# A fp32 graph-convolution kernel: two more convolution products taken in pairs of taps, and the low part of x made on GpSimd

## The reference

```python
h = relu(bn1(conv1d(xc, conv1_w)))              # one tap
h = bn2(conv1d(h, conv2_w, pad=8))              # 17 taps along the nodes
x_conv = relu(h + xc)
s = x @ w_se.T + b_se                           # 3 numbers a node
dist = sq[:, :, None] + sq[:, None, :] - 2 * s @ s.T
A = exp(-dist) * mask
x_nmp = A @ relu(x @ w_msg.T + b_msg)
x_in = concat([x_conv, x_nmp])
r, z = sigmoid(x_in @ w_ih + x @ w_hh ...)      # a GRU cell
n = tanh(gi_n + r * gh_n)
out = layernorm(x + (1 - z) * n + z * x)
```

## Time and profile before

| | us |
|---|---|
| median of 3 runs | 299.93 |
| lowest, highest | 299.28, 303.88 |
| the profiled execution, its own time | 299.77 |
| its span, first to last instruction | 297.9 |
| one round of the loop (first residual transpose to the next round's, 68.55 to 138.38) | 69.8 |

### The profile page before, as it was taken

How to read it: one execution, slowest core, us unless ns; L and a number is a source line. 1 busy time by engine, 2 the same in 40 slices (tenths; PEclk the granted TensorE clock), 3 DMA queues, 4 the chain that set the end, 5 groups by cost and what they waited for, 6 DMA issues and landing times.

```text
span 297.9 us, 4862 instructions
## 1 busy us (share of the span) xinstructions
PE 290.2 (97%) x1464; PEld 238.2 (80%) x1464; DVE 230.5 (77%) x648; ACT 198.7 (67%) x441; POOL 24.2 (8%) x50
## 2 busy tenths in 40 slices
PE   8999999999999999999999999999999999999992
PEld 6787787888887988888887888887888898887881
DVE  2799899599969966459979986449978996625795
ACT  2889656488866678378775769368884759715444
POOL 3100000000000240000000070000000033000113
PEclk9999999999999999999999999999999999999998
DMA  7502436422003323702213122721211041420002
GB/s 251 217 0 74 142 141 185 169 70 66 23 32 97 111 86 98 265 12 67 70 35 106 69 72 85 247 91 70 70 35 35 0 141 70 119 93 0 2 35 106
DMA packets 12257, 27.23 MB, mean 91 GB/s; under 512 B 1363, under 2 KB 2133, under 8 KB 12117
## 3 DMA queue, kind: packets, MB, share of 16 engines
q1 hardware_dynamic: 11956, 26.03, 26.2%
q10 hardware_dynamic: 288, 1.05, 1.1%
HBM read 22.88 MB, written 4.19 MB: 91 GB/s over the span
## 4 chain that ended last, share of the span: by engine, by line
PE 92%; DVE 4%; ACT 1%; issue 1%; POOL 1%; POOLq 0%; DVEq 0%
PE bank L357 89%; PE bank L615 2%; PE bank L410 1%; DVE first L1302 1%; DVE xr L1514 0%; DVE xr L1519 0%; ACT hn L938 0%; DVE first L1308 0%; POOL rstd L1018 0%; DVE xn L1315 0%; POOLq L84 0%; POOL rstd L1065 0%; DVE hn L1507 0%; DVE hn L1331 0%; ACT z L935 0%
## 5 line engine op out<-in xcount | busy, mean ns | idle before, releaser
L357 PE MATMUL bank<-x_hi,w_hl 128*128 128x512 f32 (+1 forms) x122 | 44.5, 405 | 0.0
L357 PE MATMUL bank<-ec_hi,w_hl 128*128 128x512 f32 (+1 forms) x98 | 35.7, 391 | 0.0
L357 PE MATMUL bank<-m_hi,w_hl 128*128 128x512 f32 (+1 forms) x98 | 35.4, 394 | 0.0
L357 PE MATMUL bank<-V_hi,cw_hi 128*128 128x512 f32 x68 | 28.6, 421 | 0.3 <-ACT bank L790 0.3
L357 PEld LDWEIGHTS bank<-x_hi,w_hl 128*128 128x128 f32 x122 | 23.0, 188 | 5.3 <-DVE x_lo L1160 0.5
L357 PE MATMUL bank<-V_lo,cw_hi 128*128 128x512 f32 x68 | 27.2, 399 | 0.0
L357 PE MATMUL bank<-V_hi,cw_lo 128*128 128x512 f32 x68 | 27.1, 398 | 0.0
L1499 DVE SCALAR_TENSOR_TENSOR hn<-xr,hn 128x512 f32<-128x512 f32 x15 | 10.4, 691 | 18.4 <-ACT hn L926 18.4
L1016 POOL TENSOR_TENSOR rstd<-first,pconst 128x4 f32<-128x4 f32 x15 | 3.4, 229 | 260.7 <-DVE first L1308 260.7
L357 PE MATMUL bank<-x_lo,w_hl 128*128 128x512 f32 (+1 forms) x61 | 23.8, 391 | 0.0
L790 ACT ACTIVATE bank<-bank 128x512 f32<-128x512 f32 x24 | 13.6, 581 | 15.1 <-PE bank L357 10.7
(11 more groups left out here) (165 smaller groups left out, 750.0 us busy)
## 6 DMA issues: line engine op xcount, KB each, us to landing
adj<-adj_dram SPq DMA_DIRECT2D x16, 512.0 KB, 4.9
x<-xt_dram SPq DMA_DIRECT2D x16, 256.0 KB, 3.2
xn<-xn_dram SPq DMA_DIRECT2D x16, 256.0 KB, 4.8
...
```

What stands on the lines that cost most here:

```text
L357: return nc.tensor.matmul(out, lhs, rhs, start=start, stop=stop, skip_group_check=True)
```

## The change

1. F2 and F3 (n = 7, 8) are split as E1 and E3 are, in the groups after the first. `T_hi`, `T_lo` get four slots, `V_hi`, `V_lo` keep two. `third(g, 2)` and `third(g, 3)` (six matmuls of 256 columns each) stand behind n = 5 on PE, into one bank; `halves` does n = 7 and 8. The differences that they need are two operations a chunk on POOL (`third_rows`), with a high part on ACT (`late_hi_f`) and a low part on DVE (`late_lo_f`). ACT keeps both thirds in `hn` (`keep_thirds`), and DVE's `add_third` puts shared bank plus third in each side bank, in place of two ACT copies.
2. In the loop POOL makes x_lo of the next group (`split_x`), in place of DVE. The first group's stays with DVE.
3. To make room: the sums `m_hi`, `m_lo` of pairs 0 and 1 lie in `T_hi`, `T_lo` once n = 3 and 5 are done, `P1` is always `hn`, `idn4` takes `bias_rows`' place, and `rstd` and `shift` lie in `mv`. The first mix stage sums F2's and F3's taps in pairs on DVE and ACT. The first loads of xn, and the two of xs behind them, wait for that (`tw_ready` 2).

The core of the diff:

```diff
-NE, NF4, NT = 3, 4, 2
+NE, NV, NT, NTE = 3, 2, 4, 2
+THIRD = {7: 0, 8: 1, 5: 2, 6: 3}
...
-            sp.wait_ge(cw_ready, NP)
+            sp.wait_ge(tw_ready, 2)
             for k in range(NC):
                 load_xn(0, k)
...
             def conv1(g, k):
-                pe.wait_ge(x_ready, 4 * g + k + 1)
+                pe.wait_ge(xlow_ready, 4 * g + k - 3)
...
+                if n >= 7 and not first:
+                    halves(n, extra, side_bank[n - 7])
+                    return
...
+                    elif n == 5:
+                        pe.wait_ge(exp_ready, 8 * g + 5)
+                        pe.wait_ge(vc_ready, 4 * g)
+                        third(g, 2)
+                        third(g, 3)
...
             def late_hi(g, k):
-                nc.scalar.activation(V_hi[:, :, k * QS:(k + 1) * QS], EF[:, k % 2, 4:8, :], ACT.Copy)
+                nc.scalar.activation(V_hi[:, :, k * QS:(k + 1) * QS], EF[:, k % 2, 4:6, :], ACT.Copy)
...
+            def keep_thirds(g):
+                act.wait_ge(third_done, 4 * g)
+                act.wait_ge(t_step, 4 * g + 4)
+                nc.scalar.activation(hn[:, 0, :], dist_bank[0][:, :], ACT.Copy).then_inc(thirds_kept, 1)
+            def late_hi_f(g, k):
+                act.wait_ge(third_ready, 4 * g + k - 3)
+                nc.scalar.activation(T_hi[:, NTE:, k, 0:QS], EF[:, k % 2, 6:8, :], ACT.Copy)
+                nc.scalar.activation(T_hi[:, NTE:, k, QS:QS + HQ - 2], next_diff(k), ACT.Copy).then_inc(vchi_ready, 1)
...
+                weights(g, 7)
                 sums_hi(g, 1)
-                weights(g, 7)
+                keep_thirds(g)
                 relu2(g, 0)
-                shared(g, 2, 0)
                 normalise_rows(g - 1, 2)
                 normalise_rows(g - 1, 3)
-                shared(g, 2, 1)
...
+            def third_rows(g, k):
+                pool.wait_ge(f_step, 4 * g + k + 1)
+                even, odd = EF[:, k % 2, 6:8, 0:HQ], EF[:, k % 2, 6:8, HQ:]
+                nc.gpsimd.tensor_tensor(next_diff(k), even[:, :, 2:], odd[:, :, 0:HQ - 2],
+                                        ALU.subtract).then_inc(odd_step, 1)
+                pool.wait_ge(odd_step, 4 * g + k + 1)
+                nc.gpsimd.tensor_tensor(even, even, odd, ALU.subtract).then_inc(third_ready, 1)
+            def split_x(g, k):
+                pool.wait_ge(xhi_ready, 4 * g + k + 5)
+                nc.gpsimd.tensor_tensor(chunk(x_lo, k), xs[:, k % 2], f32(chunk(x_hi, k)),
+                                        ALU.subtract).then_inc(xlow_ready, 1)
...
             def late_differences_f(g, k):
-                TT(EF[:, k % 2, 7, :], EF[:, k % 2, 3, :], first_e, ALU.subtract)
-                TT(EF[:, k % 2, 4:7, :], EF[:, k % 2, 0:3, :], EF[:, k % 2, 1:4, :], ALU.subtract).then_inc(f_step, 1)
+                TT(nodes_apart(e[7]), nodes_woven(e[3]), nodes_woven(first_e), ALU.subtract)
+                TT(nodes_apart(e[6]), nodes_woven(e[2]), nodes_woven(e[3]), ALU.subtract)
+                TT(EF[:, k % 2, 4:6, :], EF[:, k % 2, 0:2, :], EF[:, k % 2, 1:3, :], ALU.subtract).then_inc(f_step, 1)
...
+            def late_lo_f(g, k):
+                dve.wait_ge(vchi_ready, 4 * g + k - 3)
+                TT(T_lo[:, NTE:, k, 0:QS], EF[:, k % 2, 6:8, :], f32(T_hi[:, NTE:, k, 0:QS]), ALU.subtract)
+                TT(T_lo[:, NTE:, k, QS:QS + HQ - 2], next_diff(k), f32(T_hi[:, NTE:, k, QS:QS + HQ - 2]),
+                   ALU.subtract).then_inc(vc_ready, 1)
+            def add_third(g, side):
+                dve.wait_ge(conv2_done, NP * g + 6)
+                dve.wait_ge(thirds_kept, g)
+                dve.wait_ge(t_ready, 4 * g + side + 1)
...
+                TT(out, own, odd.broadcast_to([P, CH // 4, 2, 2]), ALU.add).then_inc(copy_ready, 1)
...
                 norm_shift(prev, 3)
+                late_lo_f(g, 2)
+                late_lo_f(g, 3)
                 mask(g, 4)
...
-                    if not last and k == 0:
-                        split_x(g + 1, 0, False)
...
-                        if k < NC - 1:
-                            split_x(g + 1, k + 1, False)
                         d_lo(g + 1, k)
+                        if k == 2:
+                            late_lo_f(g + 1, 0)
+                            late_lo_f(g + 1, 1)
```

More of the change, by code:

```diff
@@ L620, in gates_final @@
                 k = NC - 1
-                xk, mk, ck = ((chunk(a, k), chunk(b, k)) for a, b in ((x_hi, x_lo), (m_hi, m_lo), (c_hi, c_lo)))
+                xk, mk, ck = ((f(a, k), f(b, k)) for f, a, b in ((chunk, x_hi, x_lo), (pair_sums, m_hi, m_lo), (chunk, c_hi, c_lo)))
                 def part(out, w, v, start=False, stop=False):
@@ L802, in half @@
                 act.wait_ge(conv2_done, NP * g + SIDES[side] + 1)
-                if side == 0 and not first:
-                    act.wait_ge(vb_ready, 4 * g)
-                P1 = P1_first if first else P1_later
                 nc.scalar.activation(P1[:, side, :], side_bank[side][:, :], ACT.Identity, bias=v(SH2),
@@ L878, in mix_stage @@
                 half(g, 0, first)
+                late_hi_f(g, 2)
                 pre(g, 0)
@@ L936, in gru_stage @@
                                              scale=0.5).then_inc(z_ready, 1)
+                    if not last and k in (1, 2):
+                        late_hi_f(g + 1, k - 1)
                     act.wait_ge(narg_ready, 4 * g + k + 1)
@@ L967, in tap_hi, with pair_taps_hi @@
                 nc.scalar.activation(dst, src, ACT.Copy, scale=-1.0 if f % 2 else 1.0).then_inc(cwhi_ready, 1)
+            def pair_taps_hi():
+                act.wait_ge(tsum_ready, 2)
+                for i in (2, 3):
+                    last = nc.scalar.activation(tw_hi[:, 2 * i:2 * i + 2, :], tap_pairs(i)[:, :, 0], ACT.Copy,
+                                                scale=-1.0 if i % 2 else 1.0)
+                last.then_inc(twhi_ready, 1)
             def gates_hi():
```

149 lines of the change are left out of this document (97 added, 52 removed).

## The result

| | before | after |
|---|---|---|
| median, us | 299.99 (4 runs) | 303.28 (4 runs, 302.56 to 304.36) |
| profiled execution, its own time | 299.77 | 304.36 |
| its span; mean granted clock | 297.9; 0.996 | 302.5; 0.990 |

The ratio is 1.011, with a 95% interval of 1.0088 to 1.0132: 3.3 us slower, where 1.2 us faster was forecast, and just above the range.

The account below looks back on a forecast made before the run. PE's full queue was taken as the bound. From the profiled 299.77 us: -3.9 (split), +2.1 (x_lo, chunk 3), +0.6 (late_lo), together -1.2, gave 298.6 us, range 295.7 to 302.5.

Parts of the forecast that it names:

- The split: F2 and F3 on PE: 5.87 us out, 4.57 in, a gain of 1.30 a round, 3.9 in three.
- x_lo's length on POOL: A 512-column subtraction on GpSimd takes 1.3 us, between DVE's 0.69 and 2.7 from GpSimd's widest row.
- Its effect at chunk 3 alone: PE at conv1 of chunk 3: x_lo 0.6 later, 0.2 waiting beside DVE, less 0.1 slack: 0.7 a round, 2.1 in three.
- the path from DVE to x_hi of chunk 3: Tanh, messages and x_hi on ACT behind DVE's narg of chunk 2: no cost in the sum, 0.8 a round in one rival.
- the rival that ended above before: GpSimd's twelve operations block DVE: 2.7 us a round of stalls, 304.0 us; 22% for above 300, centred near 302.
- have DVE save 0.28 and pay 0.07 a chunk: Differences on DVE: shorter `late_lo` saves 0.28 a chunk, `late_differences_f` costs 0.07; 0.4 ahead by the last `late_lo`.
- The row of 0.34 us: Same four-column GpSimd operation, 1.35 us beside busy DVE, 1.01 beside idle: 0.34 read as GpSimd waiting for DVE.
- Chunks 1 and 2: x_lo on POOL ahead of conv1 there: 1.3 + 0.34 fits in the 1.7 us available, so no stall.
- The late loads: First xs loads, some 5 us later, for conv1 at 59: nothing taken, up to 0.5 us once.
- The thirds: PE at the mix stage's thirds, behind `late_lo` with DVE held by GpSimd: 0.2 us stall a round, 0.6 in three.
- The first mix stage's four new DVE operations: 256 columns each, about 1.4 us near that stage's end: covered, with 0.7 us left before the gates' first matmul on `ec_hi`.
- The signs: Profile signs: right if PE waits for x_lo at chunk 3 alone, 0.5 to 1.0 us; wrong if x_lo is above 1.8.

Follow-up runs that it names:

- experiment 5: The kernel before, with x_lo of chunk 3 alone moved to POOL: 301.92 us, ratio 1.0055.
- Experiment 1: The changed kernel with the two first loads of xs issued ahead of the four of xn: 301.43 us, ratio 1.0035.
- 7: The changed kernel with the first xs loads issued early and only chunk 3's x_lo back on DVE: 299.35 us, ratio 0.997.
- experiment 8: The changed kernel with the first xs loads issued early and all of x_lo back on DVE: 297.78 us, ratio 0.9919.
- experiment 6: The kernel before, with x_lo of chunks 0 to 2 on POOL and chunk 3's on DVE: 301.92 us, ratio 1.0065.
- experiment 9: The kernel of experiment 8, with POOL's rows for the thirds made by DVE too: 299.26 us, ratio 0.9977.
- experiment 12: Experiment 8's kernel, DVE's x_lo of chunks 1 and 2 ahead of the differences, chunk 3's x_hi and x_lo earlier on ACT and DVE: 295.98 us, ratio 0.9873.
- experiment 2: The changed kernel with x_lo back on DVE, late loads and POOL's rows for the thirds kept: 299.25 us, ratio 0.9963.

## Why the prediction was wrong, point by point

- **The split: right.** 1.30 us a round were forecast, 1.28 came, 12.27 for 13.55.
- **x_lo's length on POOL: right.** 1.3 was taken between bounds of 0.69 and 2.7 (the middle in proportion is 1.36); 1.27 to 1.31 came undisturbed, 1.43 in the mean over the twelve, up to 2.00. The estimate by the Trainium skill ("GPSIMD Engine Reference", 3.1 Elementwise — side-by-side cycle accounting), 1.1 and some 0.2 of start, agrees. Its effect at chunk 3 alone was forecast at 0.7 a round with the waiting beside DVE; experiment 5 gives 0.66, without any waiting (1.29 us), and 1 against 7 gives 0.65.
- **The step that failed: the path from DVE to x_hi of chunk 3, priced at nothing.** The forecast counted waiting at chunk 3's own x_lo and at `late_lo`. That DVE is held in the chunks before, and that the argument of tanh, tanh, messages and x_hi of chunk 3 come late by it, it put only into the rival that ended above before, at 0.8 a round. In the runs x_hi is 0.9 to 1.0 late in each round, and that comes on top of x_lo's length: 0.98 of the 1.63 a round of experiment 8's table. Half of the 0.98 is GpSimd's x_lo of chunks 0 to 2 (in the kernel before it stands alone in experiment 6). The other half stays with all of x_lo on DVE: it is the split's own work in the GRU stage, for which the forecast had DVE save 0.28 and pay 0.07 a chunk, with POOL's narrow operations holding DVE in the mix stage only. In the GRU stage they held it for 0.51 at chunk 0 (rows of experiment 9). The rival's 0.8 was for all twelve operations together. Which of the split's operations make the rest late was not taken apart; that their order decides, experiment 12 shows.
- **The rival.** Its mechanism was right for this path and its weight of 22% too low, but its other half, 1.2 us a round of stall at the thirds, came to 0.08, and it held nothing for the loads. That its 304.0 lies near 303.28 is luck in part. The row of 0.34 us showed POOL waiting for DVE; the other direction was set aside as unseen. The rule of the Trainium skill ("SBUF — State Buffer", Who interferes with whom), that a DVE instruction with two SBUF inputs contends with a GpSimd instruction that reads SBUF, and that whoever comes second is blocked for the whole of the first, spoke for it. The traces now agree in both directions: DVE's 0.30 becomes 1.37 beside POOL's 1.29, and POOL's 1.29 becomes 1.77 to 2.00 beside DVE. When DVE lets go they do not tell (see the end).
- **Chunks 1 and 2: half right.** "1.3 + 0.34 fits in the 1.7" held for chunk 1. POOL's x_lo of chunk 2 took 2.00 in rounds at full clock, and the piece grew by 0.36.
- **The late loads: mis-sized.** Nothing to 0.5 was forecast, once; moving them back is worth 1.85 us. That the load is "some 5 us later" was right (52.56 for 47.26 in the timeline of SP), but the chain behind its landing was not added up: x_hi 0.63, POOL's x_lo 1.27 and the hand-overs, from 58.85 to 60.88, end 2 us behind the matmul that wants them. About 1.3 of it stays with DVE's x_lo (experiment 2), 0.7 comes with POOL's. One execution lost another 1.67 us to the lower clock.
- **The thirds: too high.** 0.2 a round was forecast, 0.08 came. The first mix stage's four new DVE operations are hidden as forecast: the first matmul on ec stands at 57.43, where it was at 57.64.
- **The signs.** As forecast, PE waits for POOL's x_lo at chunk 3, and F2, F3 and their thirds take 4.6 us together. A round is 70.2 where 69.4 was forecast, and the wait 1.0 to 1.1 where 0.5 to 1.0 was. Of the signs of being wrong, x_lo above 1.8 with a stall at chunk 2 was seen.
- **Sum.** Experiment 1's three rounds are together 1.1 longer than before's (210.62 for 209.52): -1.28 (split), +1.34 (chunk 3), +0.36 (chunk 2) and +0.08 (thirds) each, less 0.1 to 0.2 at chunks 0 and 1. The loads add 1.85. That is 2.95 of the 3.3 measured. Experiment 1's trace, one execution, has another 0.23 ahead of the rounds and 0.27 behind them, whose cause is open.
